# Layer 0's attention: turned probabilities by way of VectorE's block transposes and DRAM, scaled first, with a plain fp32 value product

## The reference, cut to what matters

```python
q = einsum('btd,ndh->btnh', x, q_kernel)          # 16 heads of 128
k, v = einsum('bsd,ckdh->cbskh', x, kv_kernel)    # 8 key/value heads, each used by 2 query heads
q, k = rope(rms_norm(q, q_scale)), rope(rms_norm(k, k_scale))
mask = (j <= i) & (i - j < 128)                   # window of 128
probs = softmax(where(mask, q*ATTN_SCALE @ k, min))
enc = probs @ v
x = x + einsum('btnh,nhd->btd', enc, out_kernel)
```

## Time and profile of the kernel before

| what | us |
|---|---|
| runs shown | 686.14, 687.75, 690.43 (median 687.75) |
| the profiled execution's own time | 687.28 |
| its span in the trace | 685.4 |
| around the span | 1.9 |
| layer 0's attention in the trace | from some 15 to 268 |

### The profile page before, as it was taken

The page is one execution under the profiler, slowest core; times in us unless marked ns, Lnnn a source line. Parts: engine busy times, 40 slices in busy tenths (PEclk is TensorE's granted clock), DMA queues, the critical chain, the costliest instruction groups (busy, mean ns, idle before and its releaser), DMA issues.

```text
span 685.4 us, 16439 instructions
## 1 busy us (share of the span) xinstructions
PE 671.9 (98%) x4369; PEld 603.4 (88%) x4369; DVE 575.1 (84%) x1755; ACT 441.4 (64%) x1741; POOL 362.5 (53%) x555
## 2 busy tenths in 40 slices
PE   7999999999999998999999999999999999999998
PEld 3789999999999997888888899999999999978887
DVE  6979999899899999887875898989898988796333
ACT  4888888888798886431436666666666666764222
POOL 5998888898889873200138963415142324027000
PEclk9999999999999999999999999999999999999999
DMA  6010210101020001100024657465656555100000
GB/s 245 2 48 2 108 48 2 47 0 46 1 108 31 31 8 71 47 0 1 16 91 91 143 123 174 105 148 123 140 119 148 127 125 136 32 1 1 1 31 32
DMA packets 127117, 47.23 MB, mean 69 GB/s; under 512 B 93520, under 2 KB 122064, under 8 KB 126928
## 3 DMA queue, kind: packets, MB, share of 16 engines
q1 hardware_dynamic: 103824, 34.49, 20.8%
q10 hardware_dynamic: 23232, 12.06, 5.9%
HBM read 34.28 MB, written 12.26 MB: 68 GB/s over the span
## 4 chain that ended last, share of the span: by engine, by line
PE 85%; DVE 6%; issue 3%; ACT 3%; DMA 2%; SPq 0%; POOL 0%; ACTq 0%; DVEq 0%; POOLq 0%
PE bank L528 12%; PE bank L958 12%; PE bank L415 11%; PE bank L520 11%; PE bank L547 6%; PE bank L383 5%; PE bank L449 5%; PE bank L455 4%; PE bank L376 4%; PE bank L1032 3%; PE bank L431 3%; PE bank L470 3%; PE bank L1036 3%; DVE x L713 1%; PE bank L1052 1%
## 5 line engine op out<-in xcount | busy, mean ns | idle before, releaser
L713 DVE SCALAR_TENSOR_TENSOR x<-bank,rinv,x 128x256 f32<-128x256 f32 x256 | 121.0, 473 | 3.3 <-PE bank L415 1.0
L691 ACT ACTIVATE probs<-scores,negmax 128x128 f32<-128x128 f32 (+1 forms) x256 | 117.8, 475 | 6.7 <-DVE negmax L760 5.8
L600 ACT CAST enc_hi<-bank 128x256 fp32r<-128x256 f32 x128 | 47.8, 374 | 75.1 <-PE bank L455 68.8
L843 POOL TENSOR_TENSOR a_hi<-raw_a,zero 128x384 fp32r<-128x384 f32 (+1 forms) x60 | 44.2, 737 | 70.8 <-PE bank L547 70.8
L315 POOL TENSOR_TENSOR ln_r<-ln_ve,neg_half 128x1 f32<-128x1 f32 x26 | 17.1, 656 | 117.3 <-DVE ln_ve L289 117.3
L724 DVE TENSOR_TENSOR enc_lo<-bank,enc_hi 128x256 fp32r<-128x256 f32 x128 | 53.9, 421 | 24.7 <-PE bank L383 16.0
L415 PE MATMUL bank<-b_hi,enc_hi 128*128 128x256 f32 x256 | 73.4, 287 | 0.5 <-DVE x L713 0.5
L415 PE MATMUL bank<-b_hi,enc_lo 128*128 128x256 f32 x256 | 72.1, 282 | 0.0
L415 PE MATMUL bank<-b_lo,enc_hi 128*128 128x256 f32 x256 | 71.7, 280 | 0.0
L861 POOL TENSOR_TENSOR rot_a<-rot_a,rot_b 128x384 f32<-128x384 f32 x64 | 64.8, 1012 | 8.4 <-DVE rot_b L831 7.2
L859 POOL TENSOR_TENSOR rms_r<-meansq,neg_half 128x3 f32<-128x3 f32 x64 | 54.9, 857 | 7.4 <-DVE negmax L760 2.2
(11 more groups left out here) (185 smaller groups left out, 2368.0 us busy)
## 6 DMA issues: line engine op xcount, KB each, us to landing
shuffle<-blocks ACTq DMA_DIRECT2D x57, 192.0 KB, 2.5
arrived<-shuffle SPq DMA_DIRECT2D x228, 48.0 KB, 2.2
raw_a<-in_wa SPq DMA_DIRECT2D x40, 192.0 KB, 3.1
raw_a<-in_wa SPq DMA_DIRECT2D x9, 512.0 KB, 4.3
raw_b<-in_wb SPq DMA_DIRECT2D x16, 256.0 KB, 2.8
hid_last<-in_wax SPq DMA_DIRECT2D x2, 512.0 KB, 5.2
w_a<-in_w2t SPq DMA_DIRECT2D x1, 1024.0 KB, 4.9
raw_b<-in_wdown SPq DMA_DIRECT2D x2, 512.0 KB, 3.3
```

Source lines behind the costliest of these rows:

```text
L600: nc.scalar.copy(enc[0][:, hh, b * D:(b + 1) * D], bank[O_BANK][:, 0:D]).then_inc(s["ehi"], 1)
L691: nc.scalar.activation(probs[:, c % 4, c0:c1], scores[:, c % 2, c0:c1], ACT.Exp, bias=negmax[:, c % 2, r:r + 1], scale=-1.0, accum_out=row ...
L713: nc.vector.scalar_tensor_tensor(out=x[:, m % 8, :], in0=output_bank(m)[:, hh * D:(hh + 1) * D], scalar=rinv[:, u, r:r + 1], in1=x[:, m % ...
```

## The change

In layer 0, for units 0 to 55 (`MOVED[0]` = 56):
- VectorE makes 1/rowsum for every unit as the last thing in slot c (`dve_norm`), and ScalarE multiplies the probabilities with it, in two instructions of 128 and 256 columns, in slot c+1 (`act_scale`).
- VectorE transposes the 32x32 blocks of the scaled probabilities in slot c+1, ahead of its wait for the scores (`dve_blocks`).
- SyncE sends them to DRAM and fetches them back (`sp_slot0`): the send of unit c, then the fetch of unit c-1. TensorE's transposes, ScalarE's two copies and VectorE's low part go.
- The value product is fp32 for all units, straight from `arrived`. The split of v (L623, L836) goes.
- The output projection adds both heads in one 256-column region, VectorE adds it to x in one instruction. Two banks are used in turn for it.
- ScalarE makes the high part of the `a` weights of pairs 2 to 8 at the end of a slot (`act_weight_hi`), GpSimd only the low part.
- SyncE issues the weight loads between its sends and fetches at fixed slots (c % 8 = 4 and 7) instead of ahead of time, unrolled. `w2_a`'s load comes behind them.
- The hardware loop runs over slots 9 to 56, so `FIRST_MEANS` is 12 instead of 14. ScalarE's wait for `s_zero` moves from its beginning to the drain.

```diff
-FIRST_SLOT, LOOP_FROM, LOOP_STEP, LOOPS, LAST_SLOT = -5, (11, 9), 16, 3, 70
+FIRST_SLOT, LOOP_FROM, LOOP_STEP, LOOPS, LAST_SLOT = -5, (9, 9), 16, 3, 70
-MOVED = UNITS - 7
+MOVED = (UNITS - 8, UNITS - 7)
...
+def normalized(L, it, m):
+    return L == 0 and moved(L, it, m)
 def in_parts(L, it, m):
-    return it is not None or FIRST_SPLIT[L] <= m < SPLIT_VALUES
+    return L == 1 and (it is not None or m < SPLIT_VALUES)
...
 pe_output:
-                    need(pe, s["opadd"], it, m)
+                    need(pe, s["opadd"], it, m - 1 if L == 0 and m <= LAST_OUTPUT_PT + 1 else m)
+                one = normalized(L, it, m)
+                        cols = slice(0, D) if one else slice(h * D, (h + 1) * D)
 pe_values:
-                need(pe, s["ptev"], it, m + 1)
+                if normalized(L, it, m):
+                    need_turned(pe, L, it, m)
+                else:
+                    need(pe, s["ptev"], it, m + 1 - (MOVED[0] if L == 0 else 0))
+                there = arrived[:, m % 4, :] if moved(L, it, m) else probs_t[:, m % 2, :]
...
+        def act_scale(act, it, m):
+            if live(it, m) and moved(0, it, m):
+                need(act, s_norm, it, m + 1)
+                nc.scalar.mul(probs[:, m % 4, 0:128], probs[:, m % 4, 0:128], rinv[:, m % 16, 0:1])
+                nc.scalar.mul(probs[:, m % 4, 128:384], probs[:, m % 4, 128:384], rinv[:, m % 16, 1:2]).then_inc(s_scaled, 1)
 act_slot:
                 act_encoded(act, L, it, c - 4)
+            if L == 0:
+                act_scale(act, it, c - 1)
...
+            if L == 0:
+                act_weight_hi(act, it, c)
 dve_residual:
+                if normalized(L, it, m):
+                    if hh == 0:
+                        need(dve, s["op"], it, m + 1)
+                        nc.vector.tensor_tensor(x[:, m % 8, :], output_bank(L, m)[:, 0:D], x[:, m % 8, :],
+                                                ALU.add).then_inc(s["opadd"], 1)
+                    return
 dve_blocks:
+                if L == 0:
+                    need(dve, s_scaled, it, c + 1)
+        def dve_norm(dve, it, c):
+            if live(it, c) and moved(0, it, c):
+                need(dve, at[0]["exp"], it, 2 * c + 2, 2)
+                nc.vector.reciprocal(rinv[:, c % 16, :], rowsum[:, c % 16, :]).then_inc(s_norm, 1)
 dve_slot:
                 dve_turned_lo(dve, L, it, c - 3)
+                if L == 0:
+                    dve_blocks(dve, 0, it, c - 1)
                 dve_scores_wait(dve, L, it, c)
...
-            if L == 1:
-                dve_blocks(dve, it, c)
+            if L == 0:
+                dve_norm(dve, it, c)
+            else:
+                dve_blocks(dve, 1, it, c)
+        def act_weight_hi(act, it, c):
+            found = weight_part(0, it, c)
+            if found:
+                pair, part = found
+                slot, cs = pair % 2, slice(part * WA[0] // 4, (part + 1) * WA[0] // 4)
+                if part == 0:
+                    need_weight(act, 0, it, pair)
+                nc.scalar.copy(a_w[slot][0][:, cs], raw_a[:, slot, cs]).then_inc(at[0]["ahi"], 1)
 pool_slot:
+                if L == 0:
+                    need_pairs(pool, s["ahi"], it, done, 4)
+                    nc.gpsimd.tensor_tensor(a_w[slot][1][:, cs], raw_a[:, slot, cs], a_w[slot][0][:, cs].bitcast(F32),
+                                            ALU.subtract).then_inc(s["a"], 1)
 SyncE:
+            def sp_slot0(c):
+                if c < MOVED[0]:
+                    send_blocks(sp, 0, None, c)
+                if c >= 1:
+                    fetch_turned(0, c - 1)
+                if c % 8 == 4 and c // 8 + 3 < PAIRS + 2:
+                    load_a(0, None, c // 8 + 3, 0)
+                if c % 8 == 7 and c // 8 + 2 < PAIRS:
+                    load_b(0, None, c // 8 + 2)
```

More of the change, by code:

```diff
@@ L217, in build, with v_part @@
         turned = [turned0, sb("turned1", [P, 2, 2, 256], F32R)]
-        def v_part(L, part, slot, e):
-            if L == 0:
-                return b_w[slot][part][:, WB + e * DH:WB + (e + 1) * DH]
+        def v_part(part, slot, e):
             if e < 2:
@@ L411, in pe_output @@
                 else:
-                    need(pe, s["opadd"], it, m)
+                    need(pe, s["opadd"], it, m - 1 if L == 0 and m <= LAST_OUTPUT_PT + 1 else m)
+                one = normalized(L, it, m)
                 for h in range(2):
                     for i, (l, r) in enumerate(PASSES):
-                        mm = pe.matmul(output_bank(m)[:, h * D:(h + 1) * D], enc[l][:, h, t * P:(t + 1) * P],
-                                       b_w[slot][r][:, h * D:(h + 1) * D], start=i == 0, stop=i == 2)
+                        cols = slice(0, D) if one else slice(h * D, (h + 1) * D)
+                        mm = pe.matmul(output_bank(L, m)[:, cols], enc[l][:, h, t * P:(t + 1) * P],
+                                       b_w[slot][r][:, h * D:(h + 1) * D], start=i == 0 and not (one and h),
+                                       stop=i == 2 and not (one and h == 0))
                 mm.then_inc(s["op"], 1)
@@ L505, in pe_slot @@
                     need(pe, s["rot"], it, m - 1)
-                    if m % 2 == 0 and (it is not None or m - 2 >= FIRST_SPLIT[0]):
-                        need_pairs(pe, s["vlo"], it, (m - FIRST_SPLIT[0]) // 2, 4)
                     order = [(g, p) for g in range(NC) for p in PASSES]
@@ L621, in act_slot @@
                     need(act, s["pv"], it, m - t % 2 - 14)
-                    if t % 2 == 0 and (it is not None or m >= FIRST_SPLIT[0]):
-                        nc.scalar.copy(v_part(0, 0, m // 8 % 2, t // 2), bank[PJ_BANK + m % 2][:, 384:512])
                     nc.scalar.copy(v0[:, m // 8 % 2, t, :], bank[PJ_BANK + m % 2][:, 384:512]).then_inc(s["vev"], 1)
@@ L845, in split, with weight_part, need_weight @@
             nc.gpsimd.tensor_tensor(lo, src, hi.bitcast(F32), ALU.subtract).then_inc(s_lo, 1)
+        def weight_part(L, it, c):
+            m = c + 5
+            second = L == 1 and it is None and -2 <= c < 2
+            if second or (it is not None or 8 <= m < 64) and m % 2 == 0:
+                return (1, c + 2) if second else (m // 8 + 1, m % 8 // 2)
+            return None
+        def need_weight(eng, L, it, pair):
+            s, slot = at[L], pair % 2
+            need_pairs(eng, raw_as[L][slot], it, 16 * A_PARTS[L] * (pair // 2 + 1), 8 * A_PARTS[L])
+            need(eng, s["proj"], it, 8 * (pair - 1))
+            if L == 0 and it is None and pair == 2:
+                eng.wait_ge(s["a"], 4)
+            if L == 1:
+                need(eng, s["vproj"], it, 8 * (pair - 1))
+            if L == 1 and it is None and pair == 1:
+                eng.wait_ge(ff[0]["up"], 16)
+        def act_weight_hi(act, it, c):
[6 more added lines that the diff above has]
+                nc.scalar.copy(a_w[slot][0][:, cs], raw_a[:, slot, cs]).then_inc(at[0]["ahi"], 1)
         def pool_slot(pool, L, it, c):
@@ L1135, in act_drain0 @@
                 elif t == 2:
+                    act.wait_ge(s_zero, 1)
                     act_function_ahead(act, ACT.Silu)
@@ L1616, in sp_slot @@
                     load_b(1, None, c // 8 + 2)
+            def sp_slot0(c):
[7 more added lines that the diff above has]
+                    load_b(0, None, c // 8 + 2)
+            load_a(0, None, 1, 0)
+            load_b(0, None, 1)
+            load_a(0, None, 2, 0)
+            for c in range(MOVED[0] + 1):
+                sp_slot0(c)
+                if c == 20:
+                    load_late(0)
+            sp.dma_start(w2_a[:, :, :].rearrange("p a d -> p (a d)"), w2t).then_inc(s_w2, 16)
+            for h in range(2):
+                sp.wait_ge(at[0]["b"], 28 + 4 * h)
+                sp.dma_start(raw_b[:, h, :], wdown0[h]).then_inc(raw_bs[0][h], 16)
             for pair in range(2):
@@ L1626, in _ @@
                 load_a(1, None, 2, part)
-            for c in range(MOVED):
+            for c in range(MOVED[1]):
                 sp_slot(c)
```

162 lines of the change are left out of this document (67 added, 95 removed).

## The result

The changed kernel takes 694.04 us (median of nine runs, 692.28 to 697.98), the kernel before 687.75 us. The ratio is 1.0098, 95% interval 1.0081 to 1.0116: slower by 1%. Forecast were 686.4 us, no change that can be told, in a range of 677 to 695. The profiled execution took 695.29 us (span 693.3), that of before 687.28 (685.4).

What follows compares the result with a forecast made beforehand. VectorE's round through ScalarE, 3.87 us against TensorE's 3.67, was to set layer 0's slot. Terms of -1.9, -0.6, -1.0, +2.1 and +0.5 made -0.9 on 687.28: 686.4 us, own range 682 to 692, with rivals 677 to 695.

Steps and rivals of the forecast that it cites:

- TensorE's slot of 3.67: Layer 0: TensorE's own work per slot falls from 3.91 to 3.67 us with the changed value product.
- The round through ScalarE: Layer 0: reciprocal, multiplications, block transpose and on to the next reciprocal take 3.71 and 4.03 us, mean 3.87, setting the slot.
- 47 slots at -1.9: Layer 0's slots 11 to 57 shorten from 3.91 to 3.87 us each, -1.9 us in all.
- the transfers' round: Layer 0: the round by way of the transfers takes 7.1 us for two slots against 7.74, hidden, 0.3 us a slot to spare.
- Slots 3 to 10 at -0.6: Layer 0's early slots: TensorE has less to do, the first grow to VectorE's round, the later shrink; -0.6 us.
- Loads at +0.5: Layer 0: seven times fetches come later behind a 512 KB load; +0.5 us for all.
- Turnarounds at +2.1: Layer 0's two loop turnarounds: ScalarE's stop of 2.18 us delays VectorE, some 1.4 us each against 0.7 for both; +2.1 us.
- Residuals at -1.0: Slots 56 to 62: seven residuals are single where VectorE's list is tight; -1.0 us.
- The turned probabilities arrive late: The second rival: layer 0's value product waits for SyncE's fetch, slot 4.10 us with 1.1 us extra landing, 697 us; chance 0.20.
- TensorE stays the bound: Rival: layer 0's multiplications cost like copies, 0.59 us, slot 3.67 to 3.72, about 677.5 us; chance 0.30.
- Does less than it says: Rival: ScalarE's weight copy or GpSimd's late low part holds up TensorE, slot 3.9 to 4.0 us; within the forecast's own range.

Runs made afterwards that it cites:

- a_norm: The changed kernel with the reciprocal moved ahead of the second rotary product in VectorE's list; 692.83 us, ratio 1.0072.
- a_noscale: The changed kernel with late weights first, layer 0's loop written out and ScalarE's multiplications left out for all its units; 672.68 us, ratio 0.9788.
- b_unroll: The kernel before with layer 0's hardware loop written out for all engines; 686.62 us, ratio 0.9988.
- a_lateun: The changed kernel with the late weights loaded ahead of slot 0 and layer 0's loop written out; 686.98 us, ratio 0.9977.
- a_headfree: The changed kernel with late weights first, layer 0's loop written out and ScalarE's multiplications left out for units 0 to 7; 682.44 us, ratio 0.9931.
- a_actun: The changed kernel with layer 0's loop written out on ScalarE alone; 690.45 us, ratio 1.0041.
- a_poolhi: The changed kernel with GpSimd again making the high parts of the q, k, v weights in layer 0's slots; 691.84 us, ratio 1.0057.
- a_late: The changed kernel with layer 0's two late weight loads issued ahead of slot 0 instead of in slot 20; 693.83 us, ratio 1.0087.
- a_all: The changed kernel with late weights first, layer 0's loop written out and the reciprocal ahead of the second rotary product; 682.35 us, ratio 0.9922.

## Why the prediction was wrong, point by point

Three terms of the sum failed. The loads were taken one by one, at +0.5, and cost 3.6 us, because 1.5 MB stood ahead of one unit's send. The head was put at -0.6 and lost 3.1 us, most of it to the trip over ScalarE. The turnarounds were put at +2.1 and cost 2.4 us by medians, 4.6 in the traces. The round that the forecast built in its main part came out as said.

- **TensorE's slot of 3.67:** right. It shows as 3.66 in `a_norm` and 3.65 in `a_noscale`.
- **The round through ScalarE:** right. 3.63 and 4.05 against 3.71 and 4.03. The multiplications were taken at 0.81; measured are 0.31 from the start of the first to that of the second, and 0.49 for the second, 0.80. The Trainium skill's 0.29 + 0.49 (ScalarE: Activation LUTs, What ACT_TABLE_LOAD costs), which the forecast set beside its row, holds here to 0.02 us.
- **47 slots at -1.9:** right in the changed kernel. From number 9 to 56 it takes 190.9 us and the kernel before 184.7, so 6.1 more. Its two turnarounds are 5.5 of that, less 0.9 for those of the kernel before (184.7 against 183.9 in `b_unroll`), and slot 23 is 3.7; what is left is -2.1. With turnarounds and late loads out of both sides less is left: 182.8 us in `a_lateun` against 183.9 in `b_unroll`, -1.1, and the slot behind them gives that back. There late arrivals of up to 1.4 us, in a dozen slots, ate the gain. They come at every fifth slot there (13, 18, 23 and so on to 48), while in the changed kernel only 13 and 17 stand out by them besides 23; why is open. The 0.3 us a slot "to spare" in the transfers' round was too little for this scatter.
- **Slots 3 to 10 at -0.6:** wrong. The step said that the first slots grow to VectorE's round "while the later shrink". These eight (numbers 2 to 9) together grew by 0.9 us (29.8 to 30.7), and only one shrank by more than 0.1 us (number 6, 4.91 to 4.03). The larger part stands ahead of them, where the sum had no term: numbers 0 and 1 went from 3.41 and 2.07 us to 3.89 and 3.31. `a_headfree` shows the cause.
- **Loads at +0.5:** wrong, beside the head the largest miss. The step took each load as one of 512 KB, and did not follow `load_late`, which the change moved into slot 20 behind such a load: 1.5 MB ahead of one unit's send and fetches. It costs 3.6 us (690.58 less 686.98), with the lower clock behind it; in the traces slot 23 is 3.7 us longer than before.
- **Turnarounds at +2.1:** place and engine were right (`a_actun`). The size is right by the medians, 3.5 less 1.1 makes +2.4, and too small by the traces, 5.5 less 0.9 makes +4.6; with the loop written out TensorE waits longer for arrivals (9.3 us against 5.3), which takes back a part of the saving. The forecast kept ScalarE's stop at the 2.18 us of before; it is 3.0.
- **Residuals at -1.0:** not tested by itself. From slot 57 to the end the changed kernel is 0.7 us shorter.
- **The forecast's rivals:** "The turned probabilities arrive late" had the right event, the value product waiting for `arrived`, but as 1.1 us in every slot; it is one slot of 3.4 us and some small ones. "TensorE stays the bound" failed on its condition, multiplications at the price of copies. "Does less than it says", by the weight copy: the copy costs some 2 us, but at the turnaround and not in the slots (`a_poolhi`). GpSimd's late low part held up nothing that shows: `a_lo` waited 28.2 us in all and TensorE for it not at all in 60 to 250 us.

The sum, by the traces of the two profiled executions: head +3.1, loads +3.7, turnarounds +4.6, the other slots from 9 to 56 -2.1, from slot 57 on -0.7, and -0.6 at the start and in the two slots between these stretches. That makes 8.0 us, which is 695.29 less 687.28. By medians the change costs 6.3; the profiled execution of the changed kernel lies 1.25 us above its median, and by medians the turnarounds come to less.

694.04 us lies in the range of 677 to 695, and that is luck: the range reached so far for the second rival, whose slots of 4.10 us did not come about. The forecast's own part of it ended at 692.

## What to carry to other kernels

When a value starts to travel by DMA inside a tight pipeline, list everything that its queue issues between two of its transfers, by bytes, and look for the one slot where loads add up: the forecast said 0.5 us by the median load, the worst slot cost 3.6. A step added to a cross-engine round can be hidden in the steady slots and still cost time in the short slots at the head (2.1 us for eight units here), and it takes away slack that absorbed small delays; removing the multiplications brought 14.3 us, of which the shorter quiet slots explain only half (47 x 0.15 = 7). Before a cure is judged by one profile, compare the stretches that it does not touch: here layer 1 moved by up to 5.5 us by how two engines' instructions met.

## What the runs showed of the hardware that was not expected

- A VectorE subtraction of two SBUF inputs, 0.41 us elsewhere, lasted until 0.27 to 0.29 us after the end of the GpSimd pass into which it fell, up to 2.53 us in all. `a_late` reached layer 1's first transpose 1.1 us sooner than the changed kernel and had six such meetings above 1.1 us at the start of layer 1 in place of two.
- ScalarE's stop at a loop's turnaround is 3.0 us here, 2.7 with the DMA share halved, and at the second turnaround none without the weight copies in its part (`a_poolhi`). With the loop written out on ScalarE alone the time is that of the loop written out on all engines (690.45 and 690.58 us).
- After 3.36 us without work TensorE's granted clock was 0.57 for 4 us; in `a_lateun`, `a_all` and `a_noscale`, where no wait for arrivals is over 1.6 us, it was 1.00 there. It fell behind a shorter wait too: in `a_late` it was 0.64 from 124 to 128 us, behind a wait of 1.91 us at the turnaround.
- A pass of GpSimd over 1024 columns takes 2.40 us, four over 256 take 3.01.
